# Windowed attention rebuilt on small TensorE tiles, with the odd groups' position bias added by TensorE and a plain minimum on VectorE

## What is computed

```python
qkv = xw @ qkv_weight.T + qkv_bias
...
attn = jnp.einsum('whqd,whkd->whqk', q * scale, k)
coords = jnp.arange(WINDOW)
rel_idx = coords[:, None] - coords[None, :] + WINDOW - 1
rpb = bias_table[rel_idx]
attn = attn + jnp.transpose(rpb, (2, 0, 1))[None]
...
attn = jax.nn.softmax(attn, axis=-1)
out = jnp.einsum('whqk,whkd->wqhd', attn, v).reshape(Bb * nW, WINDOW, C)
out = out @ proj_weight.T + proj_bias
```

## Time and profile before

| | us |
|---|---|
| time, median of three runs (lowest, highest) | 1465.39 (1465.26, 1466.63) |
| the profiled execution's own time | 1466.03 |
| its span | 1464.2 |
| TensorE busy in the span | 1352.3 (92%) |
| VectorE, ScalarE, GpSimd busy | 969.7, 788.6, 569.1 |
| the page's costliest lines of stage 2: L646, L571, L608, L679, L688 | 160.3, 135.9, 132.2, 117.7, 87.6 |
| mean granted TensorE clock, as a share of 2.4 GHz | 0.949 |

### The profile page before, as it was taken

How to read it: one execution, slowest core, us unless ns; L and a number is a source line. 1 busy time by engine, 2 the same in 40 slices (tenths; PEclk the granted TensorE clock), 3 DMA queues, 4 the chain that set the end, 5 groups by cost and what they waited for, 6 DMA issues and landing times.

```text
span 1464.2 us, 42346 instructions
## 1 busy us (share of the span) xinstructions
PE 1352.3 (92%) x15300; PEld 969.4 (66%) x15300; DVE 969.7 (66%) x3518; ACT 788.6 (54%) x2105; POOL 569.1 (39%) x902
## 2 busy tenths in 40 slices
PE   6998998999999997999999998899999999969997
PEld 2446876777777776777777776456666665446665
DVE  3775776888888887687887785235555555646664
ACT  3974664556555554445545544235555555634553
POOL 5000114454445453355565554213333333225554
PEclk9988998999999998999999999569999999969999
DMA  8300000000000000000000000000000000000001
GB/s 223 74 1 0 1 1 1 1 0 0 0 0 0 0 0 1 2 2 0 0 0 0 0 0 2 0 1 1 0 0 0 0 0 1 1 1 10 15 14 23
DMA packets 9965, 13.76 MB, mean 9 GB/s; under 512 B 9008, under 2 KB 9008, under 8 KB 9392
## 3 DMA queue, kind: packets, MB, share of 16 engines
q1 hardware_dynamic: 9904, 12.93, 3.6%
HBM read 10.83 MB, written 2.10 MB: 9 GB/s over the span
## 4 chain that ended last, share of the span: by engine, by line
PE 75%; DVE 11%; issue 6%; ACT 6%; POOL 1%; DMA 1%; DVEq 0%; ACTq 0%; POOLq 0%; SPq 0%
PE bank L608 7%; PE bank L1267 6%; PE bank L571 6%; PE bank L1604 4%; PE bank L1622 4%; PE bank L145 4%; PE bank L1261 4%; PE bank L583 3%; PE bank L956 3%; PE bank L1226 3%; PE bank L1291 2%; PE bank L983 2%; PE bank L323 2%; PE bank L164 2%; PE bank L1369 2%
## 5 line engine op out<-in xcount | busy, mean ns | idle before, releaser
L512 POOL TENSOR_TENSOR big<-big,cst 128x512 f32<-128x512 f32 x128 | 131.9, 1062 | 131.7 <-DVE big L669 131.7
L646 ACT ACTIVATE big<-big 128x128 f32<-128x128 f32 x512 | 160.3, 391 | 33.6 <-DVE big L679 33.6
L679 DVE CUSTOM_DVE_ANT_0 big<-bank,cst 128x128 f32<-128x128 f32 x512 | 117.7, 285 | 43.3 <-issue 43.3
L571 PE MATMUL bank<-big 128*128 128x512 f32 x256 | 135.9, 613 | 1.7 <-POOL big L512 1.7
L608 PE MATMUL bank<-big 128*128 128x96 f32 x1024 | 132.2, 272 | 0.0
L608 PEld LDWEIGHTS bank<-big 128*128 128x128 f32 x1024 | 124.3, 192 | 0.9 <-issue 0.8
L1339 POOL TENSOR_TENSOR big<-g_a,g_b 64x64 f32 x128 | 40.1, 313 | 189.9 <-DVE g_a L1329 189.9
L878 POOL TENSOR_TENSOR big<-big 128x512 f32<-128x512 f32 x64 | 65.6, 1045 | 117.4 <-DVE big L1132 117.4
L1658 ACT ACTIVATE big<-bank 128x512 f32<-128x512 f32 x128 | 66.2, 603 | 51.9 <-PE bank L1604 51.9
L1320 DVE SCALAR_TENSOR_TENSOR g_t<-bank,cst,g_r 128x64 f32<-128x64 f32 x128 | 36.3, 283 | 85.6 <-ACT g_r L1306 85.6
L583 PEld LDWEIGHTS bank<-cst,big 128*128 128x128 f32 x512 | 62.5, 141 | 43.4 <-issue 37.6
(11 more groups left out here) (265 smaller groups left out, 3428.3 us busy)
## 6 DMA issues: line engine op xcount, KB each, us to landing
big<-x_dram SPq DMA_DIRECT2D x12, 512.0 KB, 8.2
cst<-consts_dram SPq DMA_DIRECT2D x1, 3364.5 KB, 22.8
out_dram<-h SPq DMA_DIRECT2D x8, 256.0 KB, 2.6
cst<-consts_dram SPq DMA_DIRECT2D x3, 256.0 KB
cst<-consts_dram SPq DMA_DIRECT2D x1, 279.5 KB, 3.9
cst<-consts_dram SPq DMA_DIRECT2D x8, 2.0 KB
cst<-consts_dram SPq DMA_DIRECT2D x2, 4.0 KB
```

Source lines behind the costliest of these rows:

```text
L512: nc.gpsimd.tensor_tensor(a_kz[l][:, 512 * u:512 * (u + 1)].rearrange("p (h k) -> p h k", h=4), a_k[l].unsqueeze(1).to_broadcast([128, 4, ...
L571: nc.tensor.matmul(bank(t % 2), a_q[l], a_kz[l][:, 512 * u:512 * (u + 1)], start=True, stop=True).then_inc(a_sc_r, 1)
L646: m = nc.scalar.activation(P, P, ACT.Exp, bias=a_mx[tb % 4][:, k:k + 1], scale=-1.0)
L679: m = nc.vector.tensor_tensor_reduce(a_P[t % 4][:, 128 * k:128 * (k + 1)], bank(t % 2)[:, 128 * k:128 * (k + 1)], c("a_bias", 512 * (u % 2 ...
```

## The change

Stage 2 keeps its groups and its slots, and changes what each engine does for a group.

- Scores: the keys are spread only once for four groups (a 128x512 block, `spread`), since a group's product now uses only its 32 rows (channels of four heads) of q and k: a 32-row tile of the array. Four score banks instead of two (`SBANK`). TensorE issues the scores two at a time, in the odd slots, for t + 1 and t + 2.
- Bias: for even groups as before, by VectorE's custom operation. For odd groups TensorE adds it to the same bank with a product of the identity and the 128x512 bias, and VectorE takes one plain minimum of the bank; the exps read the bank itself.
- Sums: every exp writes its row's sum (`accum_out`), VectorE takes the reciprocal from it, and POOL scales the exps by it (`normed`) before they are transposed.
- Transposes: all groups use one bank (bank 4). Even groups are copied out by VectorE, odd ones by ScalarE.
- Value products: the values are the weights, 32 columns at a time (8 used), and the transposed exps the moving side, 128 columns; four products fill the four 32-partition strips of one quarter of bank 6, already transposed. So the output's transpose falls away; ScalarE copies the whole bank (128x512) once per four groups, and the projection is eight products of 64 columns with zero-padded weights.
- The projection's bias is added to h by POOL before, and no longer by a product.
- SP loads the padded projection weights with eight small DMAs, ahead of the experts' constants.

The diff, cut to its core:

```diff
     xs, xT, a_q, a_k = lane(0, 128), lane(128, 128), lane(256, 128), lane(384, 128)
-    a_v = lane(512, 2 * 168)
-    a_kz = lane(1024, 2048)
-    a_o, a_oT = lane(5136, 128), lane(5264, 128)
+    a_v, a_kz = lane(512, 512), lane(1024, 512)
+    a_oT = lane(1536, 512)
     def four(at, cols):
         return [big[k // 2][:, at + cols * (k % 2):at + cols * (k % 2 + 1)] for k in range(4)]
-    a_P, a_PT, a_mx, a_rs = four(3072, 512), four(4096, 512), four(5120, 4), four(5128, 4)
-    a_bqs, a_pb = sb("a_bqs", [128, 1]), sb("a_pb", [128, 128])
...
+    a_P, a_PT, a_mx, a_rs, a_sm = four(3072, 512), four(4096, 512), four(5120, 4), four(5128, 4), four(5136, 4)
+    a_bqs, a_pb, a_pp, a_m4 = sb("a_bqs", [128, 1]), sb("a_pb", [128, 128]), sb("a_proj_padded", [128, 128]), sb("a_mask4", [128, 4])
...
-    def pipelined(engine, slot):
-        for t in range(8):
-            slot(0, t)
-        with engine.Fori(1, N2 - 1) as i:
+    def pipelined(engine, slot, ahead=1):
+        for i in range(ahead):
+            for t in range(8):
+                slot(i, t)
+        with engine.Fori(ahead, N2 - 1) as i:
...
+    SBANK = (0, 1, 5, 7)
+    def scores_bank(t):
+        return bank(SBANK[t % 4])
...
+            hp = h[:, bass.ds(i * 4 + 2 * l, 2), :]
+            nc.gpsimd.tensor_tensor(hp, hp, a_pb[:, :].rearrange("p (b c) -> p b c", c=C), ALU.add)
...
+            pool.wait_ge(a_k_r, i * 2 + (l + 1))
+            if l or exists(i, -1):
+                pool.wait_ge(a_sc_r, i * 8 + 4 * l)
+            nc.gpsimd.tensor_tensor(a_kz[l].rearrange("p (h k) -> p h k", h=4), a_k[l].unsqueeze(1).to_broadcast([128, 4, 128]),
+                                    a_m4[:, :].unsqueeze(2).to_broadcast([128, 4, 128]), ALU.mult).then_inc(a_kz_r, 1)
+        def normed(i, t):
+            pool.wait_ge(a_rs_r, i * 8 + (t + 1))
+            P = a_P[t % 4].rearrange("p (j k) -> p j k", j=4)
+            nc.gpsimd.tensor_tensor(P, P, a_rs[t % 4].unsqueeze(2).to_broadcast([128, 4, 128]), ALU.mult).then_inc(a_n_r, 1)
...
+        def scores(i, t):
+            l, u = t // 4, t % 4
+            if u == 0:
+                pe.wait_ge(a_q_r, i * 2 + (l + 1))
+                pe.wait_ge(a_kz_r, i * 2 + (l + 1))
+            if t >= 4 or exists(i, -1):
+                if t % 2:
+                    pe.wait_ge(a_e_r, i * 8 + (t - 3))
+                else:
+                    pe.wait_ge(a_mx_r, i * 8 + (t - 3))
+            r = slice(32 * u, 32 * u + 32)
+            m = nc.tensor.matmul(scores_bank(t), a_q[l][r, :], a_kz[l][r, :], start=True, stop=not t % 2)
+            if t % 2:
+                m = nc.tensor.matmul(scores_bank(t), eye, c("a_bias", 512, 1024), start=False, stop=True)
+            m.then_inc(a_sc_r, 1)
+        def attended(i, t):
+            l, u = t // 4, t % 4
+            if u % 2:
+                pe.wait_ge(a_pta_r, i * 4 + (t // 2 + 1))
+            else:
+                pe.wait_ge(a_ptd_r, i * 4 + (t // 2 + 1))
+            if u == 0:
+                pe.wait_ge(a_v_r, i * 2 + (l + 1))
+                pe.wait_ge(a_oT_r, i * 2 + (l + 2))
+            for j in range(4):
+                m = nc.tensor.matmul(bank(6)[32 * j:32 * j + 32, 128 * u:128 * u + 128], a_v[l][:, 128 * u + 32 * j:128 * u + 32 * j + 32],
+                                     a_PT[t % 4][:, 128 * j:128 * j + 128], start=True, stop=True)
+            m.then_inc(a_av_r, 1)
+        def project(i, l):
+            pe.wait_ge(a_oT_r, i * 2 + (l + 1))
+            pe.wait_ge(a_h_r, i * 2 + (l + 1))
+            for s in range(2):
+                for g in range(2):
+                    for half in (0, 64):
+                        m = nc.tensor.matmul(bank(3)[half:half + 64, 128 + 64 * s:192 + 64 * s],
+                                             a_oT[l][:, 128 * (2 * s + g) + half:128 * (2 * s + g) + half + 64], a_pp[:, 64 * g:64 * g + 64],
+                                             start=(g == 0), stop=(g == 1))
+            m.then_inc(a_pr_r, 1)
...
         def slot(i, t):
             l, u = t // 4, t % 4
-            if exists(i, 0):
-                if u == 0:
-                    pe.wait_ge(a_q_r, i * 2 + (l + 1))
-                pe.wait_ge(a_kz_r, i * 8 + (t + 1))
-                if t >= 2 or exists(i, -1):
-                    pe.wait_ge(a_mx_r, i * 8 + (t - 1))
-                nc.tensor.matmul(bank(t % 2), a_q[l], a_kz[l][:, 512 * u:512 * (u + 1)], start=True, stop=True).then_inc(a_sc_r, 1)
             if u == 0 and exists(i, l, N2 - 1):
                 rows(i + l, 1 - l)
             if u == 1 and exists(i, l, N2 - 1):
                 qkv(i + l, 1 - l)
+            ib, tb = back(i, t, 3)
+            if exists(ib, 0):
+                attended(ib, tb)
+            if t % 2:
+                for d in (1, 2):
+                    if exists(i, (t + d) // 8):
+                        scores(i + (t + d) // 8, (t + d) % 8)
+            if u == 0 and exists(i, -1, N2 - 1):
+                project(i, l)
             ib, tb = back(i, t, 2)
             if exists(ib, 0):
-                pe.wait_ge(a_e_r, ib * 8 + (tb + 1))
-                if tb >= 4 or exists(ib, -1):
-                    pe.wait_ge(a_o_r, ib * 8 + (tb - 3))
+                pe.wait_ge(a_n_r, ib * 8 + (tb + 1))
+                if tb % 2:
+                    pe.wait_ge(a_ptd_r, ib * 4 + (tb // 2 + 1))
+                elif tb or exists(ib, -1):
+                    pe.wait_ge(a_pta_r, ib * 4 + tb // 2)
                 for k in range(4):
-                    m = nc.tensor.transpose(bank(4 + tb % 4)[:, 128 * k:128 * (k + 1)], a_P[tb % 4][:, 128 * k:128 * (k + 1)], eye)
+                    m = nc.tensor.transpose(bank(4)[:, 128 * k:128 * (k + 1)], a_P[tb % 4][:, 128 * k:128 * (k + 1)], eye)
                 m.then_inc(a_pt_r, 1)
-            if u == 3:
-                ij, lj = (i, 0) if l else (i - 1, 1)
-                if exists(ij, 0):
-                    if exists(i, l):
-                        pe.wait_ge(a_v_r, i * 2 + (l + 2))
-                    pe.wait_ge(a_o_r, ij * 8 + (4 * lj + 4))
-                    nc.tensor.transpose(bank(2)[:, 384:512], a_o[lj], eye).then_inc(a_ot_r, 1)
-            if u == 0 and exists(i, -1, N2 - 1):
-                pe.wait_ge(a_oT_r, i * 2 + (l + 2))
-                pe.wait_ge(a_h_r, i * 2 + (l + 1))
-                nc.tensor.matmul(bank(3)[:, 128:256], a_oT[l], c("a_p"), start=True, stop=False)
-                nc.tensor.matmul(bank(3)[:, 128:256], eye, a_pb[:, :], start=False, stop=True).then_inc(a_pr_r, 1)
-            ib, tb = back(i, t, 3)
-            if exists(ib, 0):
-                pe.wait_ge(a_ptc_r, ib * 8 + (tb + 1))
-                if tb % 4 == 0:
-                    pe.wait_ge(a_v_r, ib * 2 + (tb // 4 + 1))
-                at = 168 * (tb % 4 // 2) + 36 * (tb % 2)
-                for k in range(4):
-                    m = nc.tensor.matmul(bank(4 + tb % 4)[:, 96 * k:96 * (k + 1)], a_PT[tb % 4][:, 128 * k:128 * (k + 1)],
-                                         a_v[tb // 4][:, at + 9 * k:at + 9 * k + 96], start=True, stop=True)
-                m.then_inc(a_av_r, 1)
...
-            for s in range(2):
-                m = nc.scalar.copy(a_v[l][:, 168 * s:168 * s + 72].rearrange("p (h d) -> p h d", h=8)[:, :, 0:8],
-                                   bank(2)[:, 256 + 64 * s:320 + 64 * s].rearrange("p (h d) -> p h d", h=8))
-            m.then_inc(a_v_r, 1)
+            nc.scalar.copy(a_v[l].rearrange("p (h d) -> p h d", d=32)[:, :, 0:8],
+                           bank(2)[:, 256:384].rearrange("p (h d) -> p h d", d=8)).then_inc(a_v_r, 1)
         def slot(i, t):
             l, u = t // 4, t % 4
             ib, tb = back(i, t, 1)
             if exists(ib, 0):
                 act.wait_ge(a_mx_r, ib * 8 + (tb + 1))
+                if tb % 2 and (tb >= 4 or exists(ib, -1)):
+                    act.wait_ge(a_pt_r, ib * 8 + (tb - 3))
                 for k in range(4):
                     P = a_P[tb % 4][:, 128 * k:128 * (k + 1)]
-                    m = nc.scalar.activation(P, P, ACT.Exp, bias=a_mx[tb % 4][:, k:k + 1], scale=-1.0)
+                    raw = scores_bank(tb)[:, 128 * k:128 * (k + 1)] if tb % 2 else P
+                    m = nc.scalar.activation(P, raw, ACT.Exp, bias=a_mx[tb % 4][:, k:k + 1], scale=-1.0, accum_out=a_sm[tb % 4][:, k:k + 1])
                 m.then_inc(a_e_r, 1)
...
-            if u == 3:
+            ib, tb = back(i, t, 2)
+            if tb % 2 and exists(ib, 0):
+                act.wait_ge(a_pt_r, ib * 8 + (tb + 1))
+                nc.scalar.copy(a_PT[tb % 4], bank(4)).then_inc(a_pta_r, 1)
+            if u == 2:
                 ij, lj = (i, 0) if l else (i - 1, 1)
                 if exists(ij, 0):
-                    act.wait_ge(a_ot_r, ij * 2 + (lj + 1))
-                    nc.scalar.copy(a_oT[lj], bank(2)[:, 384:512]).then_inc(a_oT_r, 1)
+                    act.wait_ge(a_av_r, ij * 8 + (4 * lj + 4))
+                    if exists(ij, -1):
```

(39 more changed lines are left out.)

76 lines of the change are left out of this document (38 added, 38 removed).

## The result

| | before | changed |
|---|---|---|
| median of the runs | 1465.33 us (4 runs, 1460.93 to 1466.63) | 1568.76 us (4 runs, 1562.25 to 1571.01) |
| span of the profiled execution | 1464.2 us | 1566.3 us |
| mean granted clock, whole span | 0.949 | 0.905 |

The changed kernel is slower: ratio 1.0704, 95% interval 1.0665 to 1.0743. That is +103 us; 1637 was forecast, with 1491 to 1730 as range. In every table here a median counts all executions, while a ratio is taken to the kernel before on the same chip and leaves out slow executions, those over 1.5% above the fastest of their kernel (only e10 has them, two of ten).

The account below looks back on a forecast made before the run. It took TensorE's queue to bound the kernel before, and a closed ring of waits the changed attention. With half the pairs at half clock, 64 x 7.875 = 504 us added 170.5 to 1466.03: 1637 us, range 1491 to 1730.

Parts of the forecast that it names:

- ring of four places: Windowed attention: waits through ScalarE's copy, its exps, VectorE's reciprocal and copy, and TensorE's products close a 6.25 us loop.
- The lap at full clock: Windowed attention: one round of the waits, covering two groups, takes 6.25 us against 5.21 before the change.
- bias product and switch: TensorE, end of a lap: odd group's bias product 0.89 us, return from small tiles to whole array 0.15.
- held clock: Rival: TensorE's clock stays full through the attention; 1532 us, between 1491 and 1604, chance 0.33.
- The fourfold pace of the Trainium skill: Rival: 4x on small tiles, value products 0.22, scores 0.45, lap 5.24, 1468 us; 0.04 including anything near today's.
- Two tiles saving little: TensorE's scores and value products: tiled rows elsewhere show little saving in short runs, 1.13 and 0.37 us for four records.
- the likeliest case: TensorE's clock falls in part or most of the attention stage; 1560 to 1741 us, chance 0.55.
- I take half the pairs: Attention stage: half of the 64 pairs run at half clock, 7.875 us a pair on average, +170.5 us.
- the 9.5 us for every pair at half clock: Attention stage: a lap at half clock takes 9.5 us; throughout the stage that gives 1741 us.
- The 1.6 us of standstill: TensorE in the attention: stands still about 1.6 us a lap, under ScalarE's copy and until VectorE's copy is done.
- Costed at nothing: Priced at zero: POOL's normalising, VectorE's minimum and missing copies, ScalarE's output copies, and eight more DMAs.
- TensorE alone as the bound: Rival: TensorE's own work sets the attention's pace, 4.51 us a pair, 1421 us, chance 0.03.

Follow-up runs that it names:

- e10: e9 without its product of no use on TensorE; 1457.45 us, ratio 0.9935 to the kernel before.
- e3: The changed kernel with VectorE's copy of the even group ahead of the next odd group's reciprocal; 1534.68 us.
- e8: e5 with the spread keys one slot earlier on GpSimd's queue and the layer norm's rstd two slots later; 1453.70 us.
- e1: The changed kernel plus products of no use, 128x256 and 128x512, where TensorE stands still; 1523.13 us.
- e11: The changed kernel with only GpSimd's moves, rows and spread keys early; 1566.64 us.
- e12: e1 with the products of no use reading only 32 rows, same columns; 1563.55 us.
- e9: e8 with every group's bias by VectorE, no bias product, and a 128x256 product of no use behind the odd group's transposes; 1440.39 us.
- e6: e5 with every group's bias added by VectorE and no bias product on TensorE; 1515.22 us.
- e5: e3 with TensorE's bias product behind odd transposes, scores ahead of even value products, and GpSimd's rows one slot earlier; 1478.19 us.

## Why the prediction was right, and where its sizes were off

- *What bounds the kernel.* Right. The ring of four places is there row by row, each step with the releaser that the prediction gave it, and opening it (e3 to e8) takes the pair from 6.83 to 5.04, clock included, with the same work on TensorE. That a second transpose bank would have opened it as well, as the prediction implies, was not tested: e8 opens it with one bank.
- *The lap at full clock: 6.25 forecast, 5.87 and 6.20 read.* Terms, forecast and measured: transposes 0.64, 0.64; ScalarE's copy 0.46, 0.48; exps with sum 1.50 and 0.03, 1.54 together; the rest to VectorE's copy 0.20, 0.10 (the copy starts before the reciprocal's record ends); that copy 0.72, 0.73; value products 0.40, 0.35; scores 1.13, 1.06; bias product and switch 1.04, 0.97. Durations taken from neighbouring stages were good to a tenth of a microsecond, even for products on tiles that no row of before had. The value of 1532 for a held clock stands against 1523 in e1.
- *The fourfold pace of the Trainium skill (TensorEngine Tiling (Array Packing), Theoretical Speedup).* The scores use two row tiles and not four, and got what two tiles give. The eight value products start to start take 0.35, between the 0.22 estimated from that rule and the 0.40 forecast. "Two tiles saving little" was a misreading of the prediction's own row: 1.13 against 1.78 one after the other is most of the way to the 0.89 of full overlap.
- *The clock.* Right that it falls in part of the stage and that this is the likeliest case. **The step that was mis-sized is "I take half the pairs"**, and with it the 9.5 us for every pair at half clock. That step puts 60% of the stage's time at the lower clock (9.5 of every 15.75 us); it was 30% (0.85 granted). The lower clock touched 30 of the 63 laps, nearly half, but seldom a whole one: laps with the projection reach 9.8 to 10.0, and behind the stage's first two laps (6.23 and 6.31, the pipeline still filling) no lap without it was at half clock throughout. The 1.6 us of standstill forecast for every lap are 1.91 in laps without the projection at full clock and only 0.37 in those with it. So the clock cost 43 us, not 105. That is why the time came to 1569 instead of 1637, at the lower edge of the likeliest case (1560 to 1741), and nearer to the sum for a held clock, 1532, than to the forecast. Half the pairs was a guess, as the prediction says, and the range of 239 us that contains the result is mostly this guess.
- *Costed at nothing.* GpSimd's places: right (e11), as long as the ring is closed. VectorE's minimum and the DMAs: none of TensorE's products waits for them in this stage. ScalarE's copy of the outputs: no idle time of the products in the changed kernel, but not free in kind, since it releases value products in a quarter's first group; it becomes a bound in e3.
- *The rivals.* TensorE alone as the bound was priced at 4.51 a pair and 1421. Opened, the ring gives 5.04, with TensorE busy for 97% of it (e8): the rival was too low by 0.5. Part of that is seen: four transposes beside tiled products take 0.58 and 0.69 from start to start in e8 where the prediction put 0.44, and the scores behind them take 1.41 in that lap. e1 and e12 show such a step at one place, 0.44 ahead of a product on all rows and 0.53 ahead of one on 32; that the changes of tiling cause the whole of it in e8 is an inference, since no run took them away.

What stays open: what exactly of TensorE's activity the clock follows. e12 against e1 shows that busy time is not all of it; e9 against e10 that half a microsecond of work more or less in each lap can decide. Standing still, work on few rows and changes of tiling were not separated further. Nor did any run give the transposes a second bank.

## What to carry to other kernels

Follow the order round every engine's queue before counting busy time: here the places in three queues, with one transpose bank that two engines empty in turn, turn five short hand-overs into one long chain, and the cure that the runs show is places in queues, not less work. When TensorE's busy share falls, price its clock as a second loss, and expect a fix to pay twice or not at all: taking a product off TensorE cost 37 us in e6, and a product of no use in a gap gained 42 to 46 in e1 and 12 to 17 in e9. After each opened wait read the timeline again, since a place worth nothing while the ring was closed (GpSimd's rows, e11) was worth 74 us once it was open (e5).

## What the runs showed of the hardware

- The clock fell although TensorE never stood still for more than 1.3 us, in a stage where it was busy for 83%. By the Trainium skill (TensorE: Matmul & The Clock Gate, HAM oscillation) it is long idle gaps that bring the clock down; here none is there, and the measurement decides. The section behind it (A second HAM failure mode: psum-queue depth-cycling) tells of short, frequent idling that does so, and with that this trace agrees. In e12 the clock fell (0.95) with no standstill over 0.22 us.
- Fillers that read 32 rows left a lower clock than fillers of 128 rows with the same columns: 0.95 in e12, busy for 97% of a lap at full clock, against 1.00 in e1, busy for 93%. The changes of tiling round them are a rival cause that no run removed.
- Two row tiles of 32 rows run side by side almost completely: four records of 512 columns in 1.06 us, and 1.91 on one tile.
- An exp with a sum starts 0.34 to 0.35 us after the one before it where it reads PSUM and 0.38 to 0.40 where it reads SBUF; each is followed by an accumulator read of about 0.22.
